# A four-layer mixer and experts network: TensorE's idle products removed, all but the first eleven

## The reference

```
layer 0  mixer: sim = relu(xn^T xn)^2 over the 256 pixels; out = sim (W x + b)
layer 1  mixer: 1x1 + 3x3 + 5x5 convolutions, distance attention, channel and spatial gates, tail
layer 2  mixer: Haar details of x -> 1x1 convolution -> doubling of the size -> batch norm -> relu
layer 3  mixer: two Gaussian differences, softmax attention over channels, a gated recall
experts: y = sum over e of w_e * (gelu(x W1_e + b1_e) W2_e + b2_e)
         (router weights w: by image in layer 0, otherwise by token; layer 0 has a layer norm behind)
norm:    (x - mean) / sqrt(var + eps) over the channels of each pixel
```

## Time and profile before

| | |
|---|---|
| median of three runs | 192.51 us (192.38 to 193.21) |
| profiled execution | 192.57 us |
| its span, first to last instruction | 190.8 us |
| mean granted TensorE clock | 0.998 |
| TensorE busy | 179.9 us (94%) |
| ScalarE, VectorE, GpSimd busy | 122.8, 116.3, 45.0 us |

### The profile page before, as it was taken

The page is one execution under the profiler, slowest core; times in us unless marked ns, Lnnn a source line. Parts: engine busy times, 40 slices in busy tenths (PEclk is TensorE's granted clock), DMA queues, the critical chain, the costliest instruction groups (busy, mean ns, idle before and its releaser), DMA issues.

```text
span 190.8 us, 3184 instructions
## 1 busy us (share of the span) xinstructions
PE 179.9 (94%) x1191; PEld 90.8 (48%) x1191; DVE 116.3 (61%) x312; ACT 122.8 (64%) x203; POOL 45.0 (24%) x62
## 2 busy tenths in 40 slices
PE   7999999999999898999999999999999997899991
PEld 2554323448879785422222256453224895353220
DVE  1386889758541654845535444487566698587565
ACT  2464997745336765676666560488775897588773
POOL 7371402000000001102984000030670022030670
PEclk9999999999999999999999999999999999999999
DMA  6999600000000000000000000000000000000001
GB/s 216 397 422 415 252 2 0 0 0 3 2 3 0 3 0 3 0 0 0 0 0 5 0 0 0 0 0 3 0 2 0 3 2 0 5 0 0 0 0 55
DMA packets 3087, 8.56 MB, mean 45 GB/s; under 512 B 520, under 2 KB 1040, under 8 KB 2944
## 3 DMA queue, kind: packets, MB, share of 16 engines
q1 hardware_dynamic: 2736, 7.73, 10.2%
q0 software_dynamic: 192, 0.50, 0.7%
q10 hardware_dynamic: 144, 0.13, 0.3%
HBM read 8.10 MB, written 0.26 MB: 44 GB/s over the span
## 4 chain that ended last, share of the span: by engine, by line
PE 72%; DVE 11%; ACT 6%; POOL 6%; issue 4%; POOLq 1%; ACTq 0%; DVEq 0%
PE bank L452 13%; PE banks L313 8%; PE banks L384 7%; PE banks L661 6%; PE banks L385 6%; POOL total L1600 6%; PE bank L324 4%; PE bank L318 4%; PE banks L367 4%; PE banks L620 2%; ACT hidden L872 2%; PE bank L354 2%; PE bank L432 2%; ACT rstd L843 1%; PE bank L395 1%
## 5 line engine op out<-in xcount | busy, mean ns | idle before, releaser
L872 ACT ACTIVATE hidden<-banks,pack_l 128x1024 f32<-128x1024 f32 x40 | 44.5, 1113 | 18.4 <-PE banks L385 17.1
L452 PE MATMUL bank<-hidden,w 128*64 128x512 f32 (+1 forms) x144 | 37.1, 593 | 0.6 <-ACT hidden L872 0.5
L1577 POOL CAST split_x<-normed 64x256 f16<-64x256 f32 x12 | 6.1, 506 | 79.8 <-DVE normed L1057 75.3
L384 PE MATMUL banks<-split_x,w_hi 128*128 128x512 f16 x64 | 24.6, 384 | 0.0
L385 PE MATMUL banks<-split_x,w_lo 128*128 128x512 f16 x64 | 24.3, 379 | 0.0
L313 PE MATMUL banks<-idle_work 128*128 128x512 bf16 x70 | 19.9, 416 | 1.2 <-DVE idle_work L1175 1.2
L839 ACT ACTIVATE squares<-bank 128x256 f32<-128x256 f32 x18 | 6.9, 384 | 17.8 <-PE bank L318 16.4
L1600 POOL TENSOR_TENSOR total<-total,term 128x512 f32<-128x512 f32 x12 | 17.1, 1425 | 1.9 <-DVE term L1152 1.3
L384 PEld LDWEIGHTS banks<-split_x,w_hi 128*128 128x128 f16 x64 | 6.2, 97 | 22.4 <-issue 13.4
L452 PEld LDWEIGHTS bank<-hidden,w 128*64 128x64 f32 x144 | 7.2, 134 | 14.1 <-issue 12.9
L1152 DVE TENSOR_TENSOR term<-relu_sim,bank 128x512 f32<-128x512 f32 x12 | 7.8, 684 | 7.8 <-PE bank L395 5.3
(11 more groups left out here) (318 smaller groups left out, 323.5 us busy)
## 6 DMA issues: line engine op xcount, KB each, us to landing
w_stage<-in_w SPq DMA_DIRECT2D x3, 512.0 KB, 12.4
w_stage<-in_w SPq DMA_DIRECT2D x1, 1024.0 KB, 8.9
conv<-in_conv SPq DMA_DIRECT2D x1, 800.0 KB, 7.1
w<-in_w SPq DMA_DIRECT2D x3, 256.0 KB, 12.6
w<-in_w SPq DMA_DIRECT2D x1, 512.0 KB, 9.6
toeplitz<-in_toeplitz SPq DMA_DIRECT2D x1, 512.0 KB, 10.4
gauss<-in_gauss SPq DMA_DIRECT2D x1, 512.0 KB, 11.7
pack_l<-in_pack_l SPq DMA_DIRECT2D x1, 469.0 KB, 11.1
```

What stands on the lines that cost most here:

```text
L384: mm(out, w1_hi[l][:, at:at + 128], split_x[h][:, :], start=True, stop=False)
L452: last = mm(out[64 * h:64 * h + 64, cut], w2[l][:, (f * NE + e) * CH:(f * NE + e + 1) * CH], hidden[v % 3][:, h * 512 + cut.start:h * 512 ...
L872: act(hidden[u % 3][:, :], both[u % 2][:, :], ACT.Gelu, bias=P(f"l{l}", "e_b1")[:, e * fc + f:e * fc + f + 1]).then_inc(S["moe_gelu"], 1)
```

## The change

Every call of `busy` is removed except the one of eleven products in front of the first norm; the two tables go with them. By the code that is 26 products of `NORM_TAIL`, 12 of `LAYER_TAIL` and 30 that were written in place, 68 of 79. All other instructions stay in their order, with their waits.

```diff
-        NORM_TAIL = [5, 2, 4, 4, 0, 4, 2, 4, 1]
-        LAYER_TAIL = [1, 5, 6, 0]
...
             def averages(k):
                 for j in range(INNER):
                     average(k, j)
-                busy(NORM_TAIL[k], bank[0][:, :])
...
                 down(units - 1)
-                busy(LAYER_TAIL[l], bank[2][:, :])
...
                 last.then_inc(S["l0_t"], 1)
-            busy(2, bank[5][:, :])
...
                 last.then_inc(S["l0_mixed"], 1)
-                if j == 0:
-                    busy(2, bank[6][:, :])
...
             for j in range(INNER):
                 center(3, j, x[2], x_ready(2))
-                busy(2, bank[0][:, :])
                 average(3, j)
-            busy(NORM_TAIL[3], bank[0][:, :])
...
             average(4, 1)
-            busy(NORM_TAIL[4], bank[0][:, :])
...
-            busy(6, bank[3][:, :])
             pe.wait_ge(S["bn_stats"], 1)
             mm(bank[4][:, 0:2], P("l2", "pair_mean"), bn[:, 6:8], start=True, stop=True).then_inc(S["bn_ps"], 1)
-            busy(11, bank[3][:, :])
             norm(6, x[5], x_ready(5))
...
             last.then_inc(S["qc_ps"], 1)
-            busy(4, bank[4][:, :])
...
                 last.then_inc(S["final_ps"], 1)
-                if j == 0:
-                    busy(1, bank[4][:, :])
```

## The result

| | before | changed |
|---|---|---|
| median of 20 executions | 192.57 us | 194.61 us |
| lowest to highest | 191.95 to 193.93 | 192.93 to 201.09 |
| profiled execution, its span | 192.57, 190.8 us | 193.75, 191.9 us |
| its mean granted clock | 0.998 | 0.982 |

The changed kernel is slower: ratio 1.0063, 95% interval 1.0039 to 1.0087. That interval leaves out every execution more than 1.5% above its kernel's fastest, which are 8 of the 20 here and none of the 20 before, so the medians (+2.0 us) say more about what the change costs.

The account below looks back on a forecast made before the run. The prediction took the chain of waits to run over TensorE in the expert stages, and between them over idle products too. Three falls of 1.2 us less 0.5 gained gave +3.1 on 192.57: 195.7 us, range 192.2 to 200.0.

Parts of the forecast that it names:

- the count of falls: Three clock falls: the batch norm's stretch, and two among norms 2 and 3, norm 7 and layer 3's mixer end.
- What it gives: Gain where real products stood behind idle ones after their data were there: 0.5 us, ends 0 and 1.0.
- Term (c): Norm 7: the blur, behind the second half's transpose, can begin earlier, at 149.1; 0.25 us gained.
- Term (b): Batch norm: its product starts 0.20 us after the aggregate ends, of which 0.1 us is gained.
- Term (a): Layer 0's mixing: the product needing the second half's squares starts 0.28 us after them; 0.15 us gained.
- The price of a fall: One clock fall, worked out at norm 6's center and average products, costs 1.2 us, ends 0.4 and 1.9.
- Rival 1: Only the batch-norm stretch loses the clock: 193.3 us, within what can be told from no change; chance 0.17.
- Rival 4: All bridged stretches fall and the clock stays down into the expert stages: six falls, 201 us; chance 0.10.

Follow-up runs that it names:

- execution j: The changed kernel once more with no edit, one of ten further profiled executions: 192.88 us.
- execution i: The changed kernel once more with no edit, one of ten further profiled executions: 198.23 us.
- first_7: Changed kernel with idle products around the batch norm and ending layer 3's mixer put back, seven instead of eleven before the first norm: 193.25 us, ratio 0.9981 to before.
- b: The changed kernel once more with no edit, one of ten further profiled executions: 192.93 us.
- d: The changed kernel once more with no edit, one of ten further profiled executions: 193.17 us.
- e: The changed kernel once more with no edit, one of ten further profiled executions: 196.52 us.
- g: The changed kernel once more with no edit, one of ten further profiled executions: 196.31 us.
- first_0: The changed kernel without the eleven idle products in front of the first norm too: 197.66 us, ratio 1.0127 to the kernel before.

## Why the prediction was wrong, point by point

The direction and the mechanism held, and the median of 194.61 lies in the range. The forecast of +3.1 us was too much against +2.0 by medians and +0.6% (1.2 us) by the ratio. The step that failed is the count of falls: three in the forecast, with two of them among norms 2 and 3, norm 7 and norm 8.

- **What it gives, 0.5 us.** Term (c) was right: from norm 7's last averages to the blur 149.60 - 146.92 = 2.68 us, before 149.40 - 146.42 = 2.98, and the step to norm 8 is 0.26 shorter. Term (b), 0.1 at the batch norm's product, was taken back: the product finds an idle engine and its result comes later, so the step behind it is 0.11 longer. In front of norm 5 0.32 was won where I had 0, and 0.17 of it lost again by the batch norm. Term (a), 0.15, shows from norm 0's to norm 1's center, 9.63 us where before needs 9.75, and is lost again at once in the profiled execution: VectorE's split of the weights took 2.19 us in place of 1.22, 1.11 of them beside GpSimd's cast. In execution j the way from norm 0's to norm 4's center is 0.14 shorter. The sum without the start and the falls is 0.01 - 0.32 + 0.17 + 0.11 - 0.26 = -0.3 us.
- **The price of a fall, 1.2 us.** 1.04 at norm 6, 0.86 at norm 8. At norm 6 the four records of the center took 0.94 more, 2.07 us and not 1.13, where 4 x 0.19 = 0.76 was reckoned. Right in size for a fall at a norm, and too low for one that runs on into the experts (1.3 on average, and 5.17 for the 13.7 us of execution i). I had bounded it by 1.9 with the argument that 4.3 us of work bring the clock back, read from the start of the trace; in execution i it stays low for 13.7 us, the last 9 of them without a pause.
- **The number of falls, three.** This is the step that failed. The batch norm's stretch fell in all eleven traces, as forecast. "Of the three other stretches I take two to fall" was wrong: norm 8's falls in eight of eleven, norms 2 and 3 and norm 7 in none. So the median execution pays at two places and not three: with the forecast's own terms 2 x 1.2 - 0.5 = +1.9 us, beside the measured +2.0. That they agree so closely is in part luck, since five of the eleven traces have more than two low stretches and three have one. I had set the three side by side because what I took to be left of their busy time was alike (45, 48 and 46%). The difference of two busy times was a poor guide to it. In the rows of the changed kernel norms 2 and 3 have 3.78 of 6.80 us (56%), norm 7 3.00 of 4.90 (61%) and the stretch in front of norm 8 2.60 of 5.50 (47%). That the emptiest of the three falls fits, but no run shows that this is the reason, and in first_7 norms 2 and 3 fall too. What the runs do show is the places: with the 22 products in front of norm 6 and norm 8 back, the loss is gone.
- **One number for all executions.** The prediction gave a count of falls as if it were a property of the kernel. The same program shows one to five low stretches and 192.9 to 198.2 us. Rival 1, the batch norm's fall alone, was given 0.17 and 193.3 us: it is what j, b and d show, at 192.9 to 193.2. A chance for each place would have been the thing to reason on.
- **Rival 4** (six falls, 201 us) was given 0.10. 5 of 20 executions took 201 us, with a mean clock of 0.937, hence 2 x 0.063 x 199.2 = 25 us at the low level. By 0.38 us for each beyond the first 3.4, that is 8 us over 193: an estimate by which the clock accounts for the time. The rival's own reason, the clock down in the expert stage "where TensorE has no slack", is what execution i shows. In which stages the 201 us lose it isn't settled: none of eleven profiles is of such an execution. With the batch norm alone emptied (12 executions) or alone refilled (12) none exceeds 197.6.

## What to carry to other kernels

Idle products are worth what the clock would lose at their place, and that is read off only by removing them place by place: here 22 of 68 carried the loss, and no longer did so alone once the start of the program was moved by four products. A high busy share over idle products says nothing. Idle products that end after the next real product's data are there are a delay, and the eleven in front of the first norm cost 0.8 us (ratio 0.9958 with seven). When a change touches the clock, take many executions and look at their spread and mean clock before their median.

## What the runs showed of the hardware that was not expected

- The same program has its clock rise at another moment of each execution: between 4.3 and 6.6 us in the twelve traces of the kernel before and the changed one. That alone moves the first norm from 5.07 to 5.84 us, which is about half of the spread of most executions of the kernel before (191.8 to 193.3).
- The kernel before, with all 79 idle products, doesn't always keep the clock either. Of its 75 executions beside the experiments 10 took 193.9 to 194.0 us at a mean clock of 0.989 or 0.990, the others 0.995 and more; 2 x 0.011 x 192.1 = 4.2 us at the low level, the end of the trace included. No profile is of such an execution, so the place is not known.
- A clock once down can stay down through dense work: 13.7 us behind the batch norm in execution i; in e and g it rose and fell again 3.4 us later. At the start of the trace of before it rose after 4.3 us of bfloat16 products. The Trainium skill, "TensorE: Matmul & The Clock Gate", section "What's actually happening", has the throttled state as the default that activity releases; the start of the trace agrees (0.42, then 0.23 us per product), but the rows of execution i show a TensorE that is busy and stays at the low level, and there the measurement decides.
- The product of two columns takes 0.38 us on an engine that was idle and 0.28 behind idle products.
- VectorE's split of the weights (128 x 1024, to float16) takes 1.22 us in each of ten traces in which GpSimd's cast of the convolution's weights has ended before it starts. In the seven in which the two overlap it takes longer the longer they do: 1.28 us for 0.21 us side by side (first_0), 1.60 for 0.52 (j), 2.19 for 1.11 (the profiled execution), 2.27 for 1.19 (i). The cast takes 1.52 us in all of them.
